# Three places of a three-stage Perceiver kernel re-ordered: the first layer's opening, the first tile's residual, and one expert hand-over

## The reference, cut to what matters

```
x = x + xattn(layernorm(x), ctx)      # layer 1
x = x + attn(layernorm(x))            # layer 2
x = x + moe(layernorm(x))             # layer 3

xattn: s = (c*w_cq + w_q) q^T + c w_c + biases     # 512 context rows q per batch
       a = softmax(s);  c2q = a q;  q2c = sum(softmax(max s) * c)
       z = [c, c2q, c*c2q, c*q2c] W_l^T + b_l      # four quarters of 512 features
attn:  causal heads (16 of 32), a convolution over 3 tokens gives new queries,
       causal heads again with the same k and v, output projection
moe:   14 experts of 512 x 1024 x 512, the two best of each token, gelu between
```

## Time and profile before

| what | before |
|---|---|
| median of 3 runs | 486.13 us (485.48 to 486.16) |
| the profiled execution | 490.43 us, span 488.6 us |
| PE busy | 452.6 us (93%) |
| DVE busy | 280.4 us (57%) |
| ACT busy | 162.3 us (33%) |
| POOL busy | 49.8 us (10%) |
| chain that ended last, by engine | PE 81%, DVE 12%, issue 2%, DMA 2% |
| mean granted TensorE clock | 0.97 |

### The profile page before, as it was taken

The page is one execution under the profiler, slowest core; times in us unless marked ns, Lnnn a source line. Parts: engine busy times, 40 slices in busy tenths (PEclk is TensorE's granted clock), DMA queues, the critical chain, the costliest instruction groups (busy, mean ns, idle before and its releaser), DMA issues.

```text
span 488.6 us, 8054 instructions
## 1 busy us (share of the span) xinstructions
PE 452.6 (93%) x3103; PEld 330.1 (68%) x3112; DVE 280.4 (57%) x555; ACT 162.3 (33%) x314; POOL 49.8 (10%) x58
## 2 busy tenths in 40 slices
PE   2797999999999999997999898999999999999983
PEld 1464665689898999986767766666666666666562
DVE  5639477874363133259565885566665555556637
ACT  4153135133332023043313443423344444333100
POOL 1300000001321111012030420000000000000062
PEclk9989899999999999999998999999999999999987
DMA  8987499004999638000613386899999999984452
GB/s 270 403 322 247 143 395 333 2 1 150 407 406 406 268 132 323 1 3 0 254 52 105 141 260 224 302 331 363 371 345 340 325 349 341 339 323 162 175 160 99
DMA packets 52382, 116.95 MB, mean 239 GB/s; under 512 B 4834, under 2 KB 4850, under 8 KB 52352
## 3 DMA queue, kind: packets, MB, share of 16 engines
q1 hardware_dynamic: 25984, 67.12, 36.8%
q10 hardware_dynamic: 24800, 44.62, 26.2%
q0 software_dynamic: 1568, 4.79, 3.1%
HBM read 93.98 MB, written 21.50 MB: 236 GB/s over the span
## 4 chain that ended last, share of the span: by engine, by line
PE 81%; DVE 12%; issue 2%; DMA 2%; POOL 1%; ACT 1%; DVEq 0%; ACTq 0%; POOLq 0%
PE banks L1780 17%; PE banks L1547 8%; PE banks L1759 5%; PE banks L1761 5%; PE banks L1760 5%; PE banks L1611 4%; PE banks L1413 3%; PE banks L1381 3%; PE banks L1414 3%; PE banks L1415 3%; PE banks L1452 3%; PE banks L1629 2%; PE banks L1400 2%; PE banks L1771 2%; PE banks L1580 2%
## 5 line engine op out<-in xcount | busy, mean ns | idle before, releaser
L1780 PE MATMUL banks<-w,A 128*128 128x512 f32 x208 | 91.4, 592 | 0.0
L670 ACT ACTIVATE A<-banks,b_sb 128x128 f32<-128x128 f32 x112 | 30.5, 383 | 115.5 <-issue 52.8
L1780 PEld LDWEIGHTS banks<-w,A 128*128 128x128 f32 x208 | 38.6, 190 | 43.6 <-issue 43.5
L1285 DVE COPY A<-banks 128x512 f32<-128x512 f32 x28 | 18.0, 686 | 68.0 <-PE banks L1761 67.8
L1213 DVE TENSOR_TENSOR w_lo<-w,w_hi 128x1024 fp32r<-128x1024 f32 x48 | 55.4, 1217 | 0.0
L1547 PE MATMUL banks<-A,w 128*128 128x128 f32 x384 | 48.1, 283 | 0.0
L603 ACT ACTIVATE w_hi<-w 128x1024 fp32r<-128x1024 f32 x48 | 47.3, 1094 | 0.8 <-ACT A L670 0.8
L1547 PEld LDWEIGHTS banks<-A,w 128*128 128x128 f32 x384 | 45.7, 198 | 0.7
L1759 PE MATMUL banks<-w_hi,xr 128*128 128x512 f32 x100 | 40.1, 401 | 1.5 <-DVE xr L1230 1.5
L1760 PE MATMUL banks<-w_lo,xr 128*128 128x512 f32 x104 | 40.5, 389 | 0.0
L1761 PE MATMUL banks<-w_hi,xr 128*128 128x512 f32 x100 | 39.0, 390 | 0.0
(11 more groups left out here) (288 smaller groups left out, 769.4 us busy)
## 6 DMA issues: line engine op xcount, KB each, us to landing
w<-in_w SPq DMA_DIRECT2D x12, 2048.0 KB, 10.1
w<-in_w ACTq DMA_DIRECT2D x12, 2048.0 KB, 10.7
rows_dram<-att ACTq DMA_DIRECT2D x1, 14592.0 KB, 43.1
A<-in_ctxT SPq DMA_DIRECT2D x8, 1024.0 KB, 10.4
A<-in_ctx SPq DMA_DIRECT2D x8, 1024.0 KB, 8.7
w<-in_w SPq DMA_DIRECT2D x6, 1024.0 KB, 6.1
rows_dram<-A ACTq DMA_DIRECT2D x13, 256.0 KB, 3.3
w<-in_wlT SPq DMA_DIRECT2D x3, 1024.0 KB, 15.1
```

Source lines behind the costliest of these rows:

```text
L670: ins = nc.scalar.activation(hT[:, u, f, :], HT[f // 4][:, tile(f % 4)], ACT.Gelu, bias=b1_sb[:, u, f:f + 1])
L1780: ins = mm(YP[:, :], hT[:, u, f, :], w2[:, u, f * D:(f + 1) * D], start=(f == 0), stop=(f == FT - 1))
```

## The change

Six moves in the order of instructions; no operation is added or removed.

```diff
@@ DVE, layer 1
             norm_others()
-            normalise(1)
+            for n in range(1, NT):
+                normalise(n)
             score_maxima(0)
             low_part(0, 1)
-            normalise(2)
-            normalise(3)
             dve.wait_ge(score_params_in, 16 * SCORE_PARAMS)
...
             low_part(3, 0)
+            score_maxima(1)
+            token_sums(1)
             low_wl(6)
             low_wl(7)
-            score_maxima(1)
-            token_sums(1)
@@ DVE, end of layer 2
             sums(2 * NT - 2)
+            finish(0)
             split_lo_ahead(0, range(2, KT))
-            finish(0)
             split_lo_ahead(1, range(2))
             choose(0)
@@ DVE, layer 3
             split_lo(2, 0, range(2), 2)
+            take_xT(2, 0)
+            take_y(0, 0, 1)
             find_last()
-            take_y(0, 0, 1)
-            take_xT(2, 0)
             take_h(2, 0)
@@ PE, layer 1
-            def project(n, part):
+            def project(n, part, ks=range(KT)):
...
-                for k in range(KT):
+                for k in ks:
...
             scores(0)
-            row_terms(0)
             for n in range(1, NT):
                 turn_normed(0, n)
+            row_terms(0)
             project_c(1)
...
             for n in range(1, NT):
-                turn_weights(n)
-                project(n - 1, 3)
+                if n == 1:
+                    project(0, 3)
+                    turn_weights(1)
+                    project(0, 1, range(2))
+                else:
+                    turn_weights(n)
+                    project(n - 1, 3)
                 attend(n)
                 turn_shares(n)
-                project(n - 1, 1)
+                project(n - 1, 1, range(2, KT) if n == 1 else range(KT))
@@ PE, end of layer 2
             outputs(before - 1, 0)
+            fill(SLOTS[before][2])
             turn_gate(0)
-            fill(SLOTS[before][2])
+            outputs(before - 1, 1)
             gate_logits(0)
-            outputs(before - 1, 1)
             scores(last, 0)
```

## The result

| what | before | changed |
|---|---|---|
| median | 486.14 us (4 runs, 485.48 to 488.27) | 473.37 us (4 runs, 472.90 to 475.07) |
| ratio | | 0.9728, 95% interval 0.9702 to 0.9754 |
| the profiled execution | 490.43, span 488.6 | 475.07, span 473.3 |
| mean granted clock in it | 0.970 | 0.986 |

The kernel is 12.8 us faster. (A median is of all runs; a ratio compares fast runs alone, without those that lie over 1.5% above the fastest run of their kernel.) The forecast was 15.0 us and 471.1, with a range of 467.5 to 477.3.

The account below looks back on a forecast made before the run. PE, busy nearly throughout, bounds the kernel, so time is won only where it idles or runs at half clock: layer 1 10.0, end of layer 2 4.0, experts 1.0, sum 15.0 us off the 486.13 median, 471.1 (range 467.5 to 477.3).

Parts of the forecast that it names:

- Gap A: Layer 1 opening: PE idles 2.52 us before the transposes of tiles 2 and 3; closing it counted as 2.4 us.
- Gap B: Layer 1, second tile: PE's `turn_weights(1)` waits 3.3 us for ACT's exponentials; the whole wait was to go.
- Transfers: Layer 1: weight quarter 1 lands at 33.2, cost taken as 0; last context half for `scores(3)` charged 0.1 us.
- Gap C: End of layer 2: PE idles 3.1 us before the gate's transposes; that part gives 4.0 us, 1.6 of it clock.
- Gap D: Experts: PE waits 1.49 us before `hidden(2)`; the change wins 1.0 us, leaving 0.5.
- The clock's rule: Layer 1, before `project_c(1)`: 0.15 us of idling is too little to lower the clock.
- The 6.0 us of the clock: Part of the 15.0 us sum owed to PE running at full clock; shrinks if other executions miss a fall.
- rival 1: Timed runs lack the clock falls, so only idle times go: 9.0 us, 477.1; chance 0.13.
- Rival 2: Another slow stretch, not aimed at, falls away: 1.5 to 3 us more, 468 to 469.6; chance 0.10.
- Rivals 4 and 5: 4: transfers absorb the gain before the end, 486, chance 0.03; 5: clock stays low up to `scores(2)`, 501, chance 0.02.

Follow-up runs that it names:

- layer 1 alone: Only the change's four moves in layer 1 (DVE and PE), against the kernel before: 478.44 us, ratio 0.9814.
- layer 2 alone: Only `finish(0)` ahead of two low halves on DVE and PE's fill and second `outputs` moved up, against the kernel before: 484.99 us, ratio 0.9949.

## Why the prediction was right, point by point

- **Gap A**: right. The wait went from 2.5 to 0.4 us (0.15 in the sum: `scores(0)`'s end and ACT each a little later), the clock stayed up.
- **Gap B**: right. No wait is left at `turn_weights(1)`; DVE reached `score_maxima(1)` at 40.75, the sum had 40.1. `scores(2)` came 9.5 us earlier, the sum had 10.1; 0.27 of the difference is the opening and 0.25 what is left of gap A. The clock stayed up, as in all eight profiles with gap B closed.
- **Transfers**: right for the last context half (0.1 us; 0.6 in layer 1 alone). Weight quarter 1 came 1.4 us after its due time, which cost nothing.
- **Gap C**: right in size up to the last `scores` (4.05 us more lead; 4.6 in the sum, 0.2 of the difference being the missing record, since I had set the start of the first mask product against the record of the second, and 0.15 the logits, 0.99 us where I had 0.84), but wrong in its cause and wrong behind it. I presented PE's fill as the cover of `finish(0)`. PE was free at 226.8 and `cn` ready at 226.1 by my own numbers, so the fill had nothing to cover: DVE alone gives the part, and PE's move adds the wait for the logits. Behind the last `scores` the slow stretch left 0.9 of the 4.0 us at the values of pass 7, and layer 2 alone gave 2.0 to 2.5 us.
- **Gap D**: right, 0.85 us of 1.0.
- **The clock's rule**: I took a short wait to be too little to lower the clock, "since gaps of 2.5 us and more stood ahead of each fall". That premise did not hold even in the profile before, whose stretch at 254 us has no gap over 0.85 us in the 20 us ahead of it, and the new one at 224.4 us has a wait of 0.3 us. That the clock stayed up at `project_c(1)` agrees with the forecast and not with its reason.
- **The 2.3 us between 471.1 and 473.4** come from the last step of the sum: "taken off the median". The 15.0 us were made from one execution that had lost more to the clock than most (0.970, where the kernel before had 0.972 to 0.984 in 17 runs on the first chip of the experiments and 0.973 to 0.983 in 11 on the third; on the second 11 of 29 runs were at 0.970 or below). The 6.0 us of the clock came out as 5.6 for that execution, by a new slow stretch and an absent one of the same length, and were too much for the median: the median moved by 2.6 us less than the profiled executions did. This is rival 1, in part: it was given 0.13 as a case in which all falls are absent, and what happens is that each is there in some executions.
- **Rival 2** came about with its opposite beside it: the slow stretch at 254 us went, and a new one appeared at 224.4. Rivals 4 and 5 did not occur.

## What to carry to other kernels

When a gap is closed from both sides, ask of each move alone whether it already closes it: here one line on the late engine did, and the move on the waiting engine took away the cover of another wait. When a total comes out right, follow the lead along the program: here a term of 4.0 us measured 0.9, and gains that nobody had forecast filled it up. Split a forecast into idle time, which every execution has, and clock, which differs between executions, and take only the idle time off a median at full value. When a profiled execution lies several microseconds above the median, ask whether it has more slow stretches, before any sum is made from it.

## What the runs showed of the hardware

With a wait of PE of 2.5 us at gap A the granted clock fell to 0.50 in five profiles and stayed at 1.00 in a sixth with the same wait at the same place. On one chip the same kernel spread over 8.3 us, with the mean clock from 0.969 to 0.986. The Trainium skill says in "TensorE: Matmul & The Clock Gate", section "What's actually happening", that the monitor which sets the clock is free-running and does not reset when a kernel starts, and that this is why the moment of warming up varies. That falls should vary for the same reason fits these profiles, but no run here tests it.
